# A graph layer on one core: residual sums moved, early pieces in halves, h in groups of four, a shorter warm-up

## What is computed

```
h = relu(layernorm(x))                       # x: 8192 x 128, no weights, eps 1e-5
out = x + 0.9 * (adj @ h) + 0.1 * h0         # adj: 8192 x 8192, h0: 8192 x 128
```

## Time and profile before

| | |
|---|---|
| time, three runs | 717.27, 717.71, 717.86 us (median 717.71) |
| the profiled execution | 718.35 us, its span 716.6 us |
| granted TensorE clock | 1.000 |
| PE busy | 707.0 us (99%) |
| DVE busy | 625.0 us (87%) |
| ACT busy | 521.3 us (73%) |
| POOL busy | 27.6 us (4%) |
| read from memory, written to it | 281.02 MB, 4.19 MB; mean 398 GB/s |

### The profile page before, as it was taken

The page is one execution under the profiler, slowest core; times in us unless marked ns, Lnnn a source line. Parts: engine busy times, 40 slices in busy tenths (PEclk is TensorE's granted clock), DMA queues, the critical chain, the costliest instruction groups (busy, mean ns, idle before and its releaser), DMA issues.

```text
span 716.6 us, 7886 instructions
## 1 busy us (share of the span) xinstructions
PE 707.0 (99%) x3076; PEld 575.3 (80%) x3076; DVE 625.0 (87%) x462; ACT 521.3 (73%) x342; POOL 27.6 (4%) x17
## 2 busy tenths in 40 slices
PE   7999999999999999999999999999999999999998
PEld 2777888888888888888888888888888888888886
DVE  3879998998999989998888888888888889888985
ACT  3878877869688796877767676676767767676773
POOL 1001102001020100200000000000000000000000
DMA  8999999999999999999999999999999999999991
GB/s 291 411 418 420 403 419 419 415 422 414 421 411 422 416 415 402 420 421 412 383 398 409 387 395 378 403 397 388 413 387 406 423 418 413 420 415 425 420 422 75
DMA packets 46117, 285.73 MB, mean 399 GB/s; under 512 B 5120, under 2 KB 5632, under 8 KB 14592
## 3 DMA queue, kind: packets, MB, share of 16 engines
q1 hardware_dynamic: 46080, 285.23, 98.2%
HBM read 281.02 MB, written 4.19 MB: 398 GB/s over the span
## 4 chain that ended last, share of the span: by engine, by line
PE 88%; DMA 4%; DVE 3%; issue 2%; ACT 1%; SPq 1%; POOL 0%; DVEq 0%; ACTq 0%
PE acc L428 16%; PE acc L429 16%; PE acc L433 16%; PE acc L417 13%; PE acc L412 13%; PE acc L406 13%; DMA raw<-wide_dram 4%; DVE a_lo L316 2%; SPq L190 1%; ACT a_hi L270 1%; POOL rstd L232 0%; ACT h_full L239 0%; DVE stats L282 0%; SPq L179 0%; DVE h_lo L308 0%
## 5 line engine op out<-in xcount | busy, mean ns | idle before, releaser
L316 DVE TENSOR_TENSOR a_lo<-raw,a_hi 128x2048 fp32r<-128x2048 f32 (+1 forms) x262 | 581.3, 2224 | 65.3 <-ACT a_hi L270 64.8
L270 ACT ACTIVATE a_hi<-raw 128x2048 fp32r<-128x2048 f32 (+1 forms) x262 | 487.7, 1865 | 175.3 <-PE acc L433 90.4
L428 PE MATMUL acc<-a_hi,h_hi 128*128 128x512 f32 x512 | 199.2, 389 | 0.0
L429 PE MATMUL acc<-a_hi,h_lo 128*128 128x512 f32 x512 | 199.2, 389 | 0.0
L406 PE MATMUL acc<-a_hi,h_hi 128*128 128x512 f32 x504 | 135.9, 390 | 3.0 <-ACT a_hi L270 3.0
L417 PE MATMUL acc<-a_lo,h_hi 128*128 128x512 f32 x504 | 135.8, 391 | 1.2 <-DVE a_lo L316 0.8
L433 PE MATMUL acc<-a_lo,h_hi 128*128 128x512 f32 x512 | 136.8, 389 | 0.0
L412 PE MATMUL acc<-a_hi,h_lo 128*128 128x512 f32 x504 | 134.8, 389 | 0.0
L406 PEld LDWEIGHTS acc<-a_hi,h_hi 128*128 128x128 f32 x504 | 94.1, 188 | 25.2 <-issue 2.9
L417 PEld LDWEIGHTS acc<-a_lo,h_hi 128*128 128x128 f32 x504 | 93.9, 188 | 23.8 <-DVE a_lo L316 4.6
L429 PEld LDWEIGHTS acc<-a_hi,h_lo 128*128 128x128 f32 x512 | 96.1, 188 | 20.0
(11 more groups left out here) (15 smaller groups left out, 26.9 us busy)
## 6 DMA issues: line engine op xcount, KB each, us to landing
raw<-tall_dram SPq DMA_DIRECT2D x128, 1024.0 KB, 8.7
raw<-wide_dram SPq DMA_DIRECT2D x118, 1024.0 KB, 9.8
raw<-wide_dram SPq DMA_DIRECT2D x16, 512.0 KB, 12.6
res_sb<-res_dram SPq DMA_DIRECT2D x16, 512.0 KB, 5.6
x_sb<-x_dram SPq DMA_DIRECT2D x15, 256.0 KB, 10.2
out_dram<-finished SPq DMA_DIRECT2D x15, 256.0 KB, 9.1
raw<-wide_dram SPq DMA_DIRECT2D x8, 256.0 KB, 6.4
out_dram<-finished SPq DMA_DIRECT2D x2, 128.0 KB, 1.8
```

The costliest lines, as they stand in the source:

```text
L270: nc.scalar.activation(a_hi[:, q % SPLIT_SLOTS, cols], raw[:, q % RAW_SLOTS, cols], ACT.Copy).then_inc(hi_ready, 1)
L316: nc.vector.tensor_tensor(a_lo[:, q % SPLIT_SLOTS, cols], raw[:, q % RAW_SLOTS, cols], a_hi[:, q % SPLIT_SLOTS, cols].bitcast(fp32), ALU.s ...
L428: nc.tensor.matmul(bank, h_hi[:, k, :], a_hi[:, slot, cols], start=(k == 0), stop=False)
L429: nc.tensor.matmul(bank, h_lo[:, k, :], a_hi[:, slot, cols], start=False, stop=False)
```

## The change

Four edits, all in tables and in how the host lays out adj.

1. **Halves.** Pieces 0 to 23 (`EARLY`) are loaded and rounded by ACT in halves; the quarters of pieces 0 and 1 are gone. The halves lie contiguous in an array of their own (`adj_early`). DVE's subtraction has its own table: halves only for pieces 2 to 5, whole from piece 6 on (before, halves up to piece 9). A whole subtraction waits for both halves of `a_hi`.
2. **h in groups of four** blocks throughout, with each step at a fixed distance ahead of piece 8u. Unit 1 of x is loaded behind piece 3 and not ahead of piece 2, and its statistics move from ahead of piece 2 to behind the subtraction of piece 3.
3. **Residuals.** Loads stood at pieces 12, 24, 36, ... and the sums at 20, 32, 44, ...; now loads stand at 44, 54, 64, ... and sums at 45, 55, 65, ... For the later eight chunks the load moves from 5 to 9 pieces ahead of the finish and the sum from 2 to 8.
4. **Warm-up.** 15 matmuls of 256 columns and not 12 of 512; the zero tile and its memset are half as wide.

```
-PARTS = {0: 4, 1: 4}
-PARTS.update({_q: 2 for _q in range(2, 10)})
+EARLY, EARLY_LOW = 24, 6
+PARTS = {_q: 2 for _q in range(EARLY)}
+LOW_PARTS = {_q: 2 for _q in range(EARLY_LOW)}
...
-GROUPS = [(0, 1), (1, 4), (4, 8), (8, 12), (12, 16)] + [(_b, _b + 8) for _b in range(16, BLOCKS, 8)]
+GROUPS = [(0, 1), (1, UNIT)] + [(_b, _b + UNIT) for _b in range(UNIT, BLOCKS, UNIT)]
...
+LOAD_X_AT = {4: 1}
+STATS_AT, AGGREGATE_AT, SHIFT_AT = {3: list(range(UNIT, 2 * UNIT))}, {3: 2}, {4: 2}
+SCALE_AT, HIGH_H_AT, LOW_H_AT = {5: (1, 0), 6: (1, 1)}, {6: 1}, {7: 1}
+for _u in range(2, UNITS):
+    _d = UNIT * QUADS * _u - 11
+    LOAD_X_AT[_d] = _u
+    for _k in range(UNIT):
+        STATS_AT[_d + _k] = [_u * UNIT + _k]
+    AGGREGATE_AT[_d + 4] = SHIFT_AT[_d + 5] = _u + 1
+    SCALE_AT[_d + 7], SCALE_AT[_d + 8] = (_u, 0), (_u, 1)
+    HIGH_H_AT[_d + 9] = LOW_H_AT[_d + 10] = _u
...
-    RES_LOAD_AT[12 + 12 * _n if _n < RES_RING else _at - 5] = _n
-    RES_SUM_AT[20 + 12 * _n if _n < RES_RING else _at - 2] = _n
-WARM_UP = 12
+    RES_LOAD_AT[44 + 10 * _n if _n < RES_RING else _at - 9] = _n
+    RES_SUM_AT[45 + 10 * _n if _n < RES_RING else _at - 8] = _n
+WARM_UP = 15
...
             def low_a(q):
-                for i, cols in parts(q):
-                    dve.wait_ge(hi_ready, split_through(q, i))
+                for i, cols in low_parts(q):
+                    dve.wait_ge(hi_ready, split_through(q, i if q in LOW_PARTS else None))
```

More of the change, by code:

```diff
@@ L25 @@
 RAW_SLOTS, SPLIT_SLOTS = 6, 3
-PARTS = {0: 4, 1: 4}
-PARTS.update({_q: 2 for _q in range(2, 10)})
-PART_SEMS = sum(PARTS.values())
+EARLY, EARLY_LOW = 24, 6
+PARTS = {_q: 2 for _q in range(EARLY)}
+LOW_PARTS = {_q: 2 for _q in range(EARLY_LOW)}
+PART = PIECE // 2
 UNIT = 4
@@ L78, in parts @@
     return [(i, slice(i * width, (i + 1) * width)) for i in range(n)]
-def part_number(q, i):
-    return sum(PARTS.get(k, 1) for k in range(q)) + i
 def split_through(q, i=None):
@@ L88, in split_through, with low_parts, low_through, low_part_of @@
     return sum(PARTS.get(k, 1) for k in range(NATIVE, q)) + own
+def low_parts(q):
+    n = LOW_PARTS.get(q, 1)
+    width = PIECE // n
+    return [(i, slice(i * width, (i + 1) * width)) for i in range(n)]
+def low_through(q, i=None):
+    own = LOW_PARTS.get(q, 1) if i is None else i + 1
+    return sum(LOW_PARTS.get(k, 1) for k in range(NATIVE, q)) + own
 def part_of(q, seg):
     return seg * PARTS.get(q, 1) // QUAD
+def low_part_of(q, seg):
+    return seg * LOW_PARTS.get(q, 1) // QUAD
 def pieces_of_chunk(c):
@@ L99, in pieces_of_chunk, with build @@
     return WIDE_PIECES + (c - WIDE + 1) * TALL_PIECES
-def build(nc, x, adj_wide, adj_tall, res, out):
+def build(nc, x, adj_early, adj_wide, adj_tall, res, out):
     fp32, fp32r, bf16 = mybir.dt.float32, mybir.dt.float32r, mybir.dt.bfloat16
@@ L126, in build @@
         var_eps = sb("var_eps", [P, BLOCKS])
-        exponent = sb("exponent", [P, 2 * UNIT])
+        exponent = sb("exponent", [P, UNIT])
         rstd = sb("rstd", [P, BLOCKS])
         shift = sb("shift", [P, BLOCKS])
-        warm = sb("warm", [P, SEG], bf16)
+        warm = sb("warm", [P, SEG // 2], bf16)
         acc = ctx.enter_context(nc.psum_tensor("acc", [P, WIDE, SEG], fp32))
         x_landed = [sem(f"x_landed{n}") for n in range(UNITS + 1)]
-        part_landed = [sem(f"part_landed{i}") for i in range(PART_SEMS)]
+        part_landed = [[sem(f"part_landed{s}_{i}") for i in range(2)] for s in range(RAW_SLOTS)]
         raw_landed = [sem(f"raw_landed{s}") for s in range(RAW_SLOTS)]
@@ L156, in landed_turn @@
         def landed_turn(q):
-            return sum(1 for k in range(q % RAW_SLOTS, q + 1, RAW_SLOTS) if k not in PARTS)
+            return sum(1 for k in range(q % RAW_SLOTS, q + 1, RAW_SLOTS) if (k in PARTS) == (q in PARTS))
         def wait_landed(engine, q, i):
             if q in PARTS:
-                engine.wait_ge(part_landed[part_number(q, i)], 16)
+                engine.wait_ge(part_landed[q % RAW_SLOTS][i], 16 * landed_turn(q))
             else:
@@ L186, in load_piece @@
                 for i, cols in parts(q):
-                    source = (adj_wide[q // QUADS, q % QUADS, :, cols] if q < WIDE_PIECES else
-                              adj_tall[(q - WIDE_PIECES) // TALL_PIECES, (q - WIDE_PIECES) % TALL_PIECES, :, cols])
-                    landed = part_landed[part_number(q, i)] if q in PARTS else raw_landed[q % RAW_SLOTS]
+                    if q in PARTS:
+                        source = adj_early[q, i, :, :]
+                    elif q < WIDE_PIECES:
+                        source = adj_wide[q - EARLY, :, :]
+                    else:
+                        source = adj_tall[q - WIDE_PIECES, :, :]
+                    landed = part_landed[q % RAW_SLOTS][i] if q in PARTS else raw_landed[q % RAW_SLOTS]
                     sp.dma_start(raw[:, q % RAW_SLOTS, cols], source).then_inc(landed, 16)
@@ L203, in _ @@
             load_x(1, 1, UNIT)
-            load_piece(1)
-            load_x(2, UNIT, 2 * UNIT)
-            for q in range(NATIVE, PIECES):
+            for q in range(1, PIECES):
                 if q in LOAD_X_AT:
@@ L354, in _ @@
             make_shift(1)
[L355 to L359, removed]
             low_h(0)
@@ L389, in _ @@
             for _ in range(WARM_UP):
-                nc.tensor.matmul(acc[:, WIDE - 1, :], warm[:, 0:P], warm[:, :], start=True, stop=True)
+                nc.tensor.matmul(acc[:, WIDE - 1, 0:SEG // 2], warm[:, 0:P], warm[:, :], start=True, stop=True)
             pe.wait_ge(first_h_ready, 1)
```

41 lines of the change are left out of this document (10 added, 31 removed).

## The result

| | before | after |
|---|---|---|
| median of four runs each | 717.77 us (717.27 to 717.86) | 712.24 us (711.84 to 712.35) |
| profiled execution, its span | 718.35, 716.6 us | 712.35, 710.7 us |
| ratio, with its 95% interval | | 0.9923 (0.9906 to 0.9941) |

What follows compares the result with a forecast made beforehand. PE, at 2.720 us a piece, was taken to bound the kernel behind piece 24, landings and one engine chain before it. PE reaching piece 24 at 78.9 for 82.17 gives 717.7 - 3.3 = 714.4 us, range 713.2 to 716.2.

Steps and rivals of the forecast that it cites:

- What bounds it: Behind piece 24 PE never waits, at 2.720 us a piece; only the 6.0 us of waits ahead and the start can move.
- The start: Transfers up to piece 2: unshown gain from longer rows in pieces 0 and 1, bounds 0 and about 1, taken as 0.3 us.
- The unit of x: Load no longer ahead of pieces 2, 3 and 4: they land 0.63 us earlier.
- Pieces 4 to 9: Step-by-step ACT, DVE and PE chain: PE begins piece 9 at 37.9 against 37.15 us, 0.75 lost through whole subtractions.
- Pieces 9 to 24: Landings come early, 1.5 us in hand at piece 13; PE waits 0.2 and begins piece 24 at 78.9 for 82.17.
- What costs nothing: More halves, powers, shifts and residual sums hide behind PE's 2.72 us a piece, with 3.0 us in hand behind piece 24.
- The sum: Whole kernel: 3.3 us gained, span from 716.6 to 713.3, median from 717.7 to 714.4.
- landings stay: Freed bytes buy nothing; PE begins piece 16 at 57.8, not 57.1, 0.7 less gained: 715.1 us; chance 0.15.
- the clock rival: PE idles before piece 0, so the passes of pieces 0 and 1 run at the lower clock: 715.5 us; chance 0.07.
- Eaten by whole subtractions: Pieces 6 to 9 each wait 0.9 us more as ACT and DVE pass delays on: 717.7, no change; chance 0.10.
- DVE the bound: Groups of four with powers of about 4 us make DVE the limit; at 4.1 us, 719.3, slower; chance 0.04.
- Better: Early stage has fewer waits, down to the landing limit 1.5 us below: 712.9 us; chance 0.06.

## Why the prediction was off, step by step

- **What bounds it**: right. PE's step behind piece 24 stayed at 2.720, and the 6.0 us between 82.17 and 76.17 came from ahead of it, 0.1 less in the span.
- **The start**: the step that failed. It read "The quarters of pieces 0 and 1 landed 0.65 apart [...], yet piece 0's last quarter came as late as 8.48; whether rows of 4 KB help there no row shows. Bounds are 0 and [...] about 1; I take 0.3." The measured size of that term is 18.93 - 15.24 - 0.63 = 3.06 us, three times the upper bound. It has two parts. The edit's own is shown in timed runs: quarters put back cost 1.9 us (1.26 of it up to PE's last piece), strides put back 1.3. The forecast of the median was 714.4 - 712.24 = 2.2 too high, and with the 0.3 that it allowed the edit has to give 2.5; 1.3 + 1.3 would do if they add up, which no run shows. The other part is that 18.93 was one execution's start; the same queue gave 17.18 in another. How the 3.06 divides between the two is open: one start for a kernel per profile doesn't give it, and against 17.18 the term is 1.3. The bound was wrong in its working too: it counted only to piece 1 and 10 us. All bytes up to piece 3 (4.2 MB and 0.5 MB of x) take 11.3 us at 1.26 us per 0.52 MB; begun at 3.0 us they end at 14.3, so a start of 18.93 had 4.6 us to lose.
- **The unit of x**, 0.63: the order of before cost 0.82 at the start, which agrees within the scatter; 0.17 of it was left at PE's piece 9.
- **Pieces 4 to 9**: right. The forecast has 37.9 - 18.0 = 19.9 us from the landing to PE's piece 9; measured 35.16 - 15.24 = 19.9. Pieces 6 and 7 waited for the whole subtraction (0.58, 0.30), which waited for ACT (1.24, 0.84). With `EARLY_LOW` at 24 the same stretch takes 33.32 - 14.61 = 18.71, so whole subtractions cost 1.2 here, by one profile of each.
- **Pieces 9 to 24**: 76.17 - 35.16 = 41.01 for 15 x 2.72 + 0.2 = 41.0. The 0.2 are the power of 2.99 us that was allowed for. The reserve was smaller than said: piece 13 landed at 43.54, wanted by 43.54 + 1.65 = 45.2, and PE began it at 46.24: 1.0 in hand, not 1.5.
- **What costs nothing**: right for the new tables. But the changed kernel is faster in its later part because both tables moved, and each undone alone loses 1.7 to 2.0. My working gave the residuals' part no number of its own, and my expectation for them then missed the load at piece 24.
- **The sum**: 713.3 for the span, measured 710.7; the start's 2.76 explains it: 2.7 less at piece 24, and 0.1 more behind PE's last piece.
- **The rivals**: "landings stay" fell (piece 13 landed 4.05 us earlier than in the earlier trace rows). Of the clock rival a part showed: the first passes of piece 0 stepped 6.75 - 5.90 = 0.85, twice the 0.43 of the others, at a granted clock of 1.00. It was three or so of the 16 passes, and with the longer warm-up, where PE began piece 0 without a gap, the time was the same (712.11). "Eaten by whole subtractions" and "DVE the bound" did not occur. "Better" was costed at 1.5 us below, by fewer waits. A time below that came, but by the start, so this rival was not right either.

## What to carry to other kernels

- The first microseconds were a stage with a bandwidth of its own here. Read GB/s us by us from the first issue, and don't take the steady rate or the gap between two landings for it; cut and lay out what is loaded first so that a transfer is large and contiguous.
- A start read in one profile can be off by more than the effect sought. Read it in several executions or kernels with the same first transfers before it enters a sum, and let the bound of an unshown term be as wide as that scatter.
- In a pipeline with little to spare, edits to the loads draw on the same reserve, and each has to be priced on its own: undone singly, either of two cost more than was computed (1.7 for 0.2, 2.0 for 0.6 to 1.1). Price a moved load at every place where it stood, and above all at the piece where the form changes from halves to whole.

## What the runs showed that was not expected

- The first transfers: the fourth and fifth us carried 74 and 244 GB/s with quarters 8 KB apart, 348 and 401 with contiguous halves, and in another profile of the same quarters piece 3 landed 1.75 us earlier.
- Whole pieces 0 and 1 brought no more: piece 3 landed at 14.73, inside the 14.6 to 15.4 of contiguous halves.
- Piece 3 landed with 0.9 MB of later transfers already moved in the kernel before and 0.5 MB in the changed one, so the mean GB/s alone doesn't say when a piece is there.
- With PE idle ahead of piece 0, its float32 passes stepped 0.85 us (7.28 to 8.13) and later 0.43 (15.02 to 15.45), with a granted clock of 1.00 in every stretch of one us up to 20 us of that kernel. The doubling has the ratio of the two levels, 1.2 and 2.4 GHz, and the record of the granted clock doesn't show it; what it comes from stays open.
